# A new order of the steps in a linear-attention phase, a three-pass output projection, and a square root split over two engines

## The reference, cut to what matters

```python
def _L0_attn_b_ref(x, Wq, Wk, Wv, Wf, Wb, A_log, dt_bias, Wg, bg, Wo, norm_w):
    q, k, v = (silu(x @ W).reshape(b, s, 16, 64) for W in (Wq, Wk, Wv))
    g = sigmoid((x @ Wf).reshape(b, s, 16, 64) - dt_bias)
    beta = sigmoid(x @ Wb)
    q, k = _l2norm(q), _l2norm(k)
    A = exp(-exp(A_log))
    def step(state, inp):
        q_t, k_t, v_t, g_t, b_t = inp
        o_t = einsum('bhd,bhde->bhe', q_t, state) * g_t
        state = A * state + b_t * (k_t outer v_t)
        return state, o_t
    o = scan(step)
    o = o * rsqrt(mean(o * o, axis=-1) + 1e-5) * norm_w
    gate = sigmoid(x @ Wg + bg)
    return (o * gate).reshape(b, s, 1024) @ Wo
```

## Time and profile before

| | |
|---|---|
| median of 3 runs | 914.47 us (914.35 to 917.34) |
| the profiled execution: own time | 915.93 us |
| its span, first to last instruction | 913.8 us |
| mean granted TensorE clock | 0.976 of 2.4 GHz |
| busy: PE / PEld / DVE / ACT / POOL | 92% / 79% / 60% / 56% / 70% |
| linear phase, steps m = 1 to 14 | from about 345 us to 836 us of the span |

### The profile page before, as it was taken

One profiled execution on the slowest core, in us unless ns is written; L12 is line 12 of the kernel. 1 busy time (PEld: TensorE's weight loads), 2 busy tenths in 40 slices (PEclk: granted clock), 3 DMA queues, 4 the chain that ended last, 5 costly groups with the idle time before them and its releaser, 6 DMA issues. The chain is left out here.

```text
span 913.8 us, 31013 instructions
## 1 busy us (share of the span) xinstructions
PE 841.7 (92%) x13152; PEld 717.5 (79%) x13152; DVE 548.9 (60%) x1247; ACT 511.6 (56%) x1105; POOL 636.4 (70%) x530
## 2 busy tenths in 40 slices
PE   4858998999797789999999999999999999998897
PEld 3648998899695678887888888888888888877786
DVE  3986566566684455655655655656556556666563
ACT  4745553565566636645646556566466467364354
POOL 3973211321455988898898898898898898988352
PEclk9998999999997889999999999999999999999999
DMA  5001000100100000000000000000000000000011
GB/s 189 25 13 34 25 12 1 31 19 1 25 1 1 1 3 3 3 3 3 3 3 2 3 4 2 3 4 2 3 3 3 4 2 3 4 1 3 3 36 57
DMA packets 19415, 12.36 MB, mean 14 GB/s; under 512 B 7760, under 2 KB 18768, under 8 KB 19024
## 3 DMA queue, kind: packets, MB, share of 16 engines
q1 hardware_dynamic: 19280, 10.39, 3.9%
HBM read 8.29 MB, written 2.10 MB: 11 GB/s over the span
## 5 line engine op out<-in xcount | busy, mean ns | idle before, releaser
L2101 POOL TENSOR_TENSOR la_scale<-la_scale,lt_mhalf 128x32 f32<-128x32 f32 x16 | 100.6, 6285 | 43.4 <-DVE la_scale L1756 43.4
L1446 PE MATMUL la_ps<-la_x_hi,w_hi 128*128 128x256 f32 x384 | 120.2, 313 | 0.4 <-ACT la_v L1897 0.4
L1447 PE MATMUL la_ps<-la_x_lo,w_hi 128*128 128x256 f32 x384 | 108.2, 282 | 0.0
L1448 PE MATMUL la_ps<-la_x_hi,w_lo 128*128 128x256 f32 x384 | 108.1, 281 | 0.0
L2061 POOL TENSOR_TENSOR la_coef<-la_ssk,lt_mhalf 128x32 f32<-128x32 f32 x16 | 87.0, 5440 | 13.8 <-DVE la_ssk L1774 13.8
L1797 DVE TENSOR_TENSOR lt_state<-la_s_ps,la_faded 128x512 f32<-128x512 f32 x62 | 42.3, 682 | 71.9 <-PE la_o_ps L1525 48.6
L1446 PEld LDWEIGHTS la_ps<-la_x_hi,w_hi 128*128 128x128 f32 x384 | 72.9, 190 | 16.0 <-issue 7.4
L531 POOL CAST at_q_hi<-qk_hi 128x128 fp32r<-128x128 f32 x32 | 9.4, 294 | 106.1 <-PE at_s_ps L572 103.6
L598 PE MATMUL at_o_ps<-V,at_probsT 128*128 128x128 f32 x544 | 75.1, 278 | 3.2 <-DVE at_probsT L507 2.0
L2079 POOL TENSOR_TENSOR la_k<-la_k,lt_decay_k 128x1024 f32<-128x1024 f32 x32 | 75.6, 2364 | 2.1 <-ACT n_xn L1953 2.1
L2086 POOL TENSOR_TENSOR la_qdT<-la_qT,lt_decay_q 128x1024 f32<-128x1024 f32 x32 | 76.3, 2384 | 0.0
(11 more groups left out here) (207 smaller groups left out, 2382.6 us busy)
## 6 DMA issues: line engine op xcount, KB each, us to landing
at_w_raw<-in_w SPq DMA_DIRECT2D x20, 128.0 KB, 2.2
X<-in_x SPq DMA_DIRECT2D x8, 256.0 KB, 2.9
out<-X SPq DMA_DIRECT2D x8, 256.0 KB, 2.3
qkv_cos<-in_cos SPq DMA_DIRECT2D x1, 1024.0 KB, 4.8
qkv_sin<-in_sin SPq DMA_DIRECT2D x1, 1024.0 KB, 7.0
lt_w_out<-in_w_out SPq DMA_DIRECT2D x4, 128.0 KB, 2.7
const<-in_const SPq DMA_DIRECT2D x1, 320.5 KB, 3.2
qkv_w<-in_w_qkv SPq DMA_DIRECT2D x1, 320.0 KB, 3.9
```

Source lines behind the costliest of these rows:

```text
L1446: eng.matmul(out, l_hi, r_hi, start=True, stop=False)
L1447: eng.matmul(out, l_hi, r_lo, start=False, stop=False)
L1448: return eng.matmul(out, l_lo, r_hi, start=False, stop=True)
L2101: eng.tensor_tensor(scale[:, :, :], scale[:, :, :], powers, ALU.pow).then_inc(s["scale_step"], 1)
```

## The change

- The order of the steps on PE is new. The small-array work of a step now stands in three groups with no projection between: (`attend(m,0,0)`, `turn_k`, `attend(m,0,1)`, `recall(m,0,0)`, `scores(m,1)`), then after `sum_squares` (`recall(m,0,1)`, `update`), and at the end (`attend(m,1,0)`, `turn_k`, `attend(m,1,1)`, `recall(m,1,0)`, `scores(m+1,0)`, `recall(m,1,1)`, `update`). The scores of the next tile's first batch row move to the end of the step before.
- `project_out` multiplies in three passes of split operands. ScalarE makes the high part of `u` (`high_u`), DVE the low part (`low_u`); `w_out` is split once.
- `invert_totals` is one GpSimd instruction, the power, into a new tile `root`; DVE makes high and low part (`split_scales`).
- `square_q` writes into the free second halves of a `k` and a `v` buffer, not into `sq`.
- The orders on DVE, ACT and POOL are rewritten to match, and so is the tail.

The diff, cut to its core:

```diff
+        ring = Ring(("f0 f1 su f2 sT f3 be k0 k1 v0 v1 kT0 kT1 s10 s11 sq sB k2 b0 b1 k3 b2 b3 v2 v3 q0 q1 q2 q3 y g0 g1 yt g2 g3 xt "
+                     "kT2 kT3 s00 s01").split(), has, STEPS, BANKS)
...
             def project_out(m):
-                for j in range(4):
-                    taken(eng, m, f"b{j}")
+                if m == 1:
+                    eng.wait_ge(s["w_lo_ready"], 1)
+                eng.wait_ge(s["ulo_ready"], 4 * m)
                 bank = free(eng, m, "y")
+                out = ps[bank][:, 0:W]
                 for c in range(NP):
-                    mm = eng.matmul(ps[bank][:, 0:W], w_out[:, c, :], u[:, c, :], start=(c == 0), stop=(c == NP - 1))
+                    eng.matmul(out, tables.w_out_hi[:, c, :], u_hi[:, c, :], start=(c == 0), stop=False)
+                    eng.matmul(out, tables.w_out_hi[:, c, :], u_lo[:, c, :], start=False, stop=False)
+                    mm = eng.matmul(out, tables.w_out_lo[:, c, :], u_hi[:, c, :], start=False, stop=(c == NP - 1))
...
             def step(m):     # PE, after; conditions on prv, now, nxt left out
+                f0 f1 su f2 turn_totals f3 betas(m + 1) k0 k1 v0 v1
+                attend(m, 0, 0) turn_k(m, 0) attend(m, 0, 1) recall(m, 0, 0) scores(m, 1)
+                sq recall(m, 0, 1) update((m, 0, 1), (m, 1, 0))
+                turn_scales(m) k2 spread_scales(m, 0) (m, 1) k3 (m, 2) (m, 3) v2 v3 q0 q1 q2 q3
+                project_out(m) g0 g1 turn_y(m) g2 g3 turn_x(m + 2)
+                attend(m, 1, 0) turn_k(m, 1) attend(m, 1, 1) recall(m, 1, 0) scores(m + 1, 0)
+                recall(m, 1, 1) update((m, 1, 1), (m + 1, 0, 0))
...
+            def split_scales(m):    # DVE
+                eng.wait_ge(s["scale_step"], ROOT_STEPS * (m - 1) + 1)
+                high = parts[:, :, 0:H]
+                eng.tensor_copy(high, root[:, :, :]).then_inc(s["scale_step"], 1)
+                eng.wait_ge(s["scale_step"], ROOT_STEPS * (m - 1) + 2)
+                eng.tensor_tensor(parts[:, :, H:2 * H], root[:, :, :], high.bitcast(F32), ALU.subtract).then_inc(s["scale_step"], 1)
...
+            def low_u(m, j):        # DVE
+                eng.wait_ge(s["uhi_ready"], 4 * (m - 1) + j + 1)
+                part = slice(2 * j, 2 * j + 2)
+                eng.tensor_tensor(u_lo[:, part, :], u[:, part, :], u_hi[:, part, :].bitcast(F32), ALU.subtract).then_inc(s["ulo_ready"], 1)
...
             def step(m):     # DVE, after; conditions left out
+                decayed(m, 0) gate_u(m - 1, 0) add_totals(m) gate_u(m - 1, 1) gather_totals(m)
+                square_q(m) normalize(m + 2) new_state(m, 0, 0) decayed(m, 1) guard_q(m) sum_k(m + 1, 0)
+                split_scales(m) new_state(m, 0, 1)
+                scale_u(m, 0) scale_u(m, 1) low_u(m, 0) scale_u(m, 2) low_u(m, 1) scale_u(m, 3) low_u(m, 2) low_u(m, 3)
+                sum_k(m + 1, 1) guard_k(m + 1) gate_o(m, 0) moments(m + 3) residual(m)
+                new_state(m, 1, 0) gate_o(m, 1) new_state(m, 1, 1)
...
+            def high_u(m, j):       # ACT
+                taken(eng, m, f"b{j}")
+                part = slice(2 * j, 2 * j + 2)
+                eng.activation(u_hi[:, part, :], u[:, part, :], ACT.Copy).then_inc(s["uhi_ready"], 1)
...
             def step(m):     # ACT, after; conditions left out
+                square_u(m - 1, 1) f0 f1 f2 f3 beta_tanh k0 k1 v0 v1 square_k(m + 1, 0) copy_kT(m, 0) (m, 1)
+                copy_scales(m) k2 k3 high_u(m, 0) (m, 1) v2 high_u(m, 2) (m, 3) v3 square_k(m + 1, 1) q0 q1 q2 q3
+                copy_y(m) square_u(m, 0) g0 g1 g2 g3 copy_x(m + 2) copy_kT(m, 2) (m, 3)
...
             def invert_totals(m):   # POOL
                 taken(eng, m, "sT")
+                if m > 1:
+                    eng.wait_ge(s["scale_step"], ROOT_STEPS * (m - 1))
                 powers = mhalf[:, :].rearrange("p (b h) -> p b h", b=B)
-                eng.tensor_tensor(scale[:, :, :], scale[:, :, :], powers, ALU.pow).then_inc(s["scale_step"], 1)
-                eng.wait_ge(s["scale_step"], 3 * m - 2)
-                high = parts[:, :, 0:H]
-                eng.tensor_tensor(high, scale[:, :, :], zeros[:, :, :], ALU.add).then_inc(s["scale_step"], 1)
-                eng.wait_ge(s["scale_step"], 3 * m - 1)
-                eng.tensor_tensor(parts[:, :, H:2 * H], scale[:, :, :], high.bitcast(F32), ALU.subtract).then_inc(s["scale_step"], 1)
+                eng.tensor_tensor(root[:, :, :], scale[:, :, :], powers, ALU.pow).then_inc(s["scale_step"], 1)
...
             def step(m):     # POOL, after; conditions left out
+                decay_queries(m, 0) decay_keys(m, 1) inverse_roots(m + 2) invert_totals(m)
+                fade(m, 1, 0) decay_queries(m, 1) decay_keys(m + 1, 0) fade(m, 0, 1) fade(m + 1, 0, 0)
+                coefficients(m + 1) weigh_v(m + 1, 0) weigh_v(m + 1, 1) fade(m, 1, 1) low_x(m + 2)
```

More of the change, by code:

```diff
@@ L1815, in step @@
                     decayed(m, 0)
-                if prv and now:
-                    new_state(m - 1, 1, 1)
                 if prv:
+                    gate_u(m - 1, 0)
                     add_totals(m)
@@ L1830, in step @@
                     ffn.moments(eng, 3)
+                if now:
+                    new_state(m, 0, 0)
+                    decayed(m, 1)
+                    guard_q(m)
                 if nxt:
@@ L1833, in step @@
                 if prv:
-                    for j in range(4):
-                        scale_u(m, j)
+                    split_scales(m)
+                if now and nxt:
+                    new_state(m, 0, 1)
+                if prv:
+                    scale_u(m, 0)
+                    scale_u(m, 1)
+                    low_u(m, 0)
+                    scale_u(m, 2)
+                    low_u(m, 1)
+                    scale_u(m, 3)
+                    low_u(m, 2)
+                    low_u(m, 3)
                 if nxt:
@@ L1858, in step @@
                     gate_o(m, 1)
-                if m == LAST - 2:
-                    ffn.moments(eng, 1)
+                if now and nxt:
+                    new_state(m, 1, 1)
+                if m == -1:
+                    split_w_out()
             for m in STEPS[:-1]:
                 step(m)
-            ffn.normalize(eng, 2)
+            gate_u(LAST, 0)
             add_totals(NT)
@@ L1868, in _ @@
             ffn.normalize(eng, 3)
+            split_scales(NT)
+            scale_u(NT, 0)
+            scale_u(NT, 1)
+            low_u(NT, 0)
+            scale_u(NT, 2)
+            low_u(NT, 1)
+            scale_u(NT, 3)
+            low_u(NT, 2)
+            low_u(NT, 3)
             ffn.output(eng, 0)
             ffn.moments(eng, 4)
-            for j in range(4):
-                scale_u(NT, j)
             ffn.output(eng, 1)
@@ L1894, in silu_token @@
                     eng.wait_ge(up_full[1], B * (m - 1) + b + 1)
+                if exists(m) and b == 1:
+                    written(eng, m, "sq")
                 bank = written(eng, m, job)
@@ L2004, in step @@
+                if m == LAST:
+                    written(eng, m, "sq")
+                    ffn.copy_x(eng, 0)
+                if prv:
+                    copy_y(m)
+                if now:
+                    square_u(m, 0)
+                    for j in range(4):
+                        gates(m, "g", j)
                 if exists(m + 2):
@@ L2027, in _ @@
             ffn.tanh(eng, 0)
+            copy_scales(NT)
             ffn.square(eng, 1)
             ffn.tanh(eng, 1)
+            for j in range(4):
+                high_u(NT, j)
             ffn.copy_x(eng, 3)
-            copy_scales(NT)
             ffn.square(eng, 2)
@@ L2111, in step @@
                     decay_queries(m, 0)
-                if now:
-                    fade(m, 0, 0)
+                    decay_keys(m, 1)
+                if now and exists(m + 2):
+                    norm.inverse_roots(eng, Tile(0, m + 2))
                 if prv:
```

272 lines of the change are left out of this document (130 added, 142 removed).

## The result

The changed kernel takes 1015.3 us (median of 4 runs, 1012.8 to 1016.54) where the kernel before takes 914.64 (4 runs, 914.35 to 917.34) on the same chip: a ratio of 1.109, 95% interval 1.106 to 1.112. It is slower, as forecast, but by 101 us instead of 57, and outside the range of 926 to 991.

What follows compares the result with a forecast made beforehand. GpSimd's list was taken to bound the kernel: 29.36 us of work, 6.85 idle and 3.2 of meetings make 39.4 us a step against 35.07. Over 14 intervals, +60.6 us, with the ends +57.1, giving 971.5 us, range 926 to 991.

Steps and rivals of the forecast that it cites:

- the 0.98 and 1.1 in the sum: GpSimd at a step's start: us added per step because two `gate_u` meet `decay_queries`, `decay_keys` and `inverse_roots`.
- sign on the faded state: Profile sign on DVE: the wait of `new_state` for `la_faded` would be larger than before the change.
- the sentence on `split_scales`: DVE's `split_scales` meets `fade` and `decay_queries`, 0.2 us, and waits up to 2.4 us, which PE can absorb.
- the ring: Experiments' loop across engines: totals' power, scales, VectorE's state and scaling, TensorE's list, back to the totals; no size.
- 29.36 + 6.85 + 3.2: GpSimd's step: own list 29.36 us, idle before the coefficients 6.85, meetings with DVE 3.2; 39.4 us together.
- PE's gain: PE's list: fewer small-array group entries and a faster output projection make it 2.5 us a step shorter.
- one thing: GpSimd's idle time before `coefficients`: under 2.5 us a step, PE's gain comes in, 881 us; chance 0.11.
- The meeting of the small instructions: DVE's `split_scales` running beside GpSimd's `fade` and `decay_queries`: 0.2 us a step.
- the clock rival: PE idles up to 3 us before `turn_scales`, its clock falls: 40.8 us a step, 991 us; chance 0.10 (above 986).
- The ends: Outside the 14 full intervals: step 0 -2 us, last step -2, tail +0.5.
- Theory B: Experiments' theory: the ring sets the step; the wait for the key sums is only where GpSimd stands meanwhile.
- the 945 and 925 us above: Expected in experiments: 945 with split on GpSimd and `new_state(m,0,1)` late; 925 with `gate_u(m,0)` also in its own step.

Runs made afterwards that it cites:

- best version: The reordered kernel with the old tail, plus `fade(m,1,1)`, `square_k(m+1,1)`, `sum_k` and `guard_k` moved earlier in their lists: 932.2 us.
- the two runs of 1039 us: Changed kernel with key sums taken early on VectorE and ScalarE, 1039.3 us; changed kernel with GpSimd held behind its root until VectorE has split it, 1039.6 us.
- the hold: GpSimd waits behind its root until VectorE has split it: changed kernel 1039.6 us; with `split_scales` also earlier on VectorE, 999.6 us.
- the reordered kernel: Changed kernel with the split on GpSimd and a new order of GpSimd's list and others: 966.0 us; with the old tail as well, 964.3 us.

## Why the prediction was wrong in size

**What held.** PE's list is not the limit any more, and PE is busy 85% of the steady steps (forecast around 80%). GpSimd idles 7.8 us a step before the coefficients (forecast 6.85), released by `guard_k`. It is hardly idle before the totals, 0.82 us. The 24 passes take 2.92 us (forecast 2.9). `gate_u` does meet GpSimd, 2.91 us in each step's first one; the key and query instructions keep 1.90 and 2.37 us beside it, and the price falls on `inverse_roots` (1.17 us at its first instruction, 0.19 in the best version), so this meeting cost GpSimd less than the 0.98 and 1.1 in the sum. The forecast had named the 1.90 and 2.39 us as the sign that it was too high; they came, and it was too low. Its sign on the faded state failed too: `new_state` waits 10.3 us in 8 for `la_faded`, where it was 12.3 in 14.

**The step that failed** is the sentence on `split_scales`: "it waits up to 2.4 us itself, which PE pays and can". PE can't. Its wait for the scales (30.6 us in 13) delays `spread_scales`, hence the first `scale_u`, and with it the rest of the ring. Taking the wait away gave 19 us (split on GpSimd) or 22 (earlier place). The earlier place lowers the step from 40.7 to 39.3 us, as much as the forecast of 39.4 was short.

The same place shows which term of the sum was too small. From F, the end of `fade(m,0,1)`, to the end of the last `scale_u` the forecast laid DVE's instructions in a row, 4.45 us. The trace has F at 604.99 and that end at 611.72: 6.7 us, of which DVE waits 0.74 for PE's spread and 1.23 for `high_u`. The rest, ACT's part and the key sums, takes 3.6 us as forecast, and `guard_k` ends at 615.28: 10.3 us after F instead of 8.1. GpSimd's waits in this step (592.46 to 633.61, 41.15 us) are then 0.87 + 8.24 + 0.82 = 9.9 us where 6.85 were forecast, and its own list is 31.2 us where 29.36 + 3.2 = 32.6 were. A term that was too large hid part of one that was too small; that the step of 39.4 came as near as it did is luck to that extent.

**The reason given for the step was wrong too**, and only experiments could tell. The forecast made the sum 29.36 + 6.85 + 3.2 of GpSimd's list and its wait, and held that whether PE's gain comes in "is decided by one thing", the idle time before `coefficients`. Four runs change that wait and contradict it: it fell from 80.4 to 16.7 us in all with the time unchanged; it halved in one run and fell from 101.5 to 81.9 in another, and both got 24 us slower, with the clock lower too; with state and split both moved it went to 4.5, and the step still was 38.0 us because GpSimd waited for VectorE's state instead (60.9 us in 15). A sum over one engine's list and its waits always gives the length of the step, whichever engine is taken; it says nothing on which of the waits would give time back.

**PE's gain** was put at 2.5 us a step. In the best version PE's busy time is 476.84 us in 514.0 / 35.78 = 14.4 steps, 33.2 a step against 34.2: 1.0 us came. Where the rest of the seven saved group entries went was not measured. (The forecast's 0.7 us for the projection is 0.8 by its own rows, 3.72 less 2.9.)

**The meeting of the small instructions** was in the forecast at 0.2 us of GpSimd's time for `split_scales`. In the changed kernel VectorE's subtraction is stretched by 1.64 us at the place shown (1.83 less 0.19), and in the kernel before the meeting alone makes 51 us. By the Trainium skill, page "SBUF — State Buffer", section "Who interferes with whom", the loser of the shared ports is blocked for the whole instruction; the cast's 2.33 us beside a 2.36 us `decay_queries` agree. The same section of the Trainium skill's page counts a cast among the instructions that can take the ports, when its operands meet conditions; here a 128x32 cast from float32 to float32r does.

**The clock** was a rival at 0.10, with a stall of PE before `turn_scales` and a step of 40.8 us. The stall is there, and the measured mean is 40.8. Windows at two of the places, 41 us apart, show the clock near its lower level, 0.50 or 1.2 GHz (columns as above):

```profile
603.80:607.30 3.50, 3.20 (x11) 2.82 (x12) 1.63 (x3) 0.98 (x2) 2.45 (x4) 0.56 0.00 0
644.80:648.30 3.50, 3.06 (x11) 2.67 (x12) 1.63 (x3) 0.98 (x2) 2.59 (x4) 0.55 0.00 0
```

The stretch begins as PE ends its 2.18 us wait for the scales, so it follows from the same wait. The mean of the steady steps is 0.98: 2% of 555 us, some 11 us at most. Over the whole span it is 0.958 where it was 0.976: 4.2% of 1010.5 us less 2.4% of 913.8, some 20 of the 97 us at most. Both are estimates, and no run isolates the clock. From 366 to 880 us it is 0.93 and 0.94 in the two runs of 1039 us, 0.96 to 0.98 in those from 996 to 1015, and 0.98 to 1.00 in the faster ones. So each change of an order above carries a share of it, the 6 us between the two runs with the earlier split (0.99 and 0.96) too, and the clock rival is not excluded as a part of the cause.

**The ends.** Start and last step were put at -2 each and measured +2.1 and +5.2. The tail was put at +0.5 and measured +8.7; with the old order of the tail 5.9 of it go. The last interval falls from 35.0 to 31.0 once the split is back on GpSimd; with the split earlier on VectorE it stays at 35.0, and with the hold as well it is 31.9. So it hangs on the stretched split, not on its place. The start was not looked into.

**Misses while explaining.** Theory B names the right engines but doesn't give sizes. Besides the 945 and 925 us above, the reordered kernel was expected at 915 to 935 and took 964 to 966; the new order with one plain pass was expected at 980 to 992 and took 1010; the root split in the kernel before at 940 to 955 and took 967; and the hold in the changed kernel came out 22 us above the slowest time of its three theories. The gains were added up as if each wait were by itself. What is shown is which moves give time back, down to 932 us; that one ring sets the step is the reading that fits them, and 16 us stay unexplained.

## What to carry to other kernels

A wait in the profile, even one of the longest, released at the same place in each step, is a candidate and no cause: remove it in a copy of the kernel and see whether the step gets shorter. Where each engine works through a written list, follow the ring across engines (here root, scales, state, scaling, TensorE, totals) and ask of each small hand-over what stands ahead of it in the receiving list and what GpSimd instruction starts beside it. Before a tiny instruction is moved from GpSimd to VectorE, price it at the length of GpSimd's next instruction; a short wait that keeps GpSimd still can be far cheaper, but only if VectorE gets to the work at once.

## What was not expected of the hardware

- A 128x32 cast on VectorE that takes 0.18 us undisturbed lasted 2.33 us when it started 0.07 us behind a 2.36 us GpSimd instruction, in most steps; two such instructions of 0.37 us together made a kernel 51 us (5.6%) longer, and a 0.52 us wait on GpSimd undid it.
- GpSimd's `pow` of 128x32 takes 6.34 us when it starts next to VectorE's `square_q` and 5.46 otherwise; the same 6.34 stand in the changed kernel, although `square_q` there writes to other buffers.
- Removing a wait of GpSimd, or a stretched VectorE instruction, twice made the kernel slower by 24 us, and in both runs the granted clock of TensorE was lower, 0.94 and 0.93 where the changed kernel has 0.98.
